# A modulated filter chain on one core: the blur taken out of the filter's matmuls

## The reference

```python
def _layer(x, style, w, b, mw, mb, typ):
    s = style @ mw.T + mb
    weight = SCALE * w * s[:, None, :, None]
    demod = lax.rsqrt(jnp.sum(weight * weight, axis=(2, 3)) + EPS)
    weight = weight * demod[:, :, None, None]
    if typ == 'same':
        out = jax.vmap(_conv_same)(x, weight) + b[None, :, None]
    elif typ == 'upsample':
        out = jax.vmap(_conv_up)(x, weight.transpose(0, 2, 1, 3)) + b[None, :, None]
        out = _blur(out, 2.0 * blur_k, (1, 1))
    elif typ == 'downsample':
        xb = _blur(x, blur_k, (2, 2))
        out = jax.vmap(_conv_down)(xb, weight) + b[None, :, None]
    return out
# types in order: same, upsample, same, downsample; blur_k = [1, 3, 3, 1] / 8
```

## Time and profile before

| | us |
|---|---|
| median of three runs | 1350.0 |
| the profiled execution, first to last instruction | 1349.2 |
| TensorE busy in it | 1342.2 |
| VectorE busy | 1077.1 |
| ScalarE busy | 818.2 |
| GpSimd busy | 330.2 |
| DMA moved | 141.32 MB, mean 105 GB/s |

### The profile page before, as it was taken

The page is one execution under the profiler, slowest core; times in us unless marked ns, Lnnn a source line. Parts: engine busy times, 40 slices in busy tenths (PEclk is TensorE's granted clock), DMA queues, the critical chain, the costliest instruction groups (busy, mean ns, idle before and its releaser), DMA issues.

```text
span 1349.2 us, 20544 instructions
## 1 busy us (share of the span) xinstructions
PE 1342.2 (99%) x7013; PEld 1128.4 (84%) x7013; DVE 1077.1 (80%) x1798; ACT 818.2 (61%) x1407; POOL 330.2 (24%) x633
## 2 busy tenths in 40 slices
PE   8999999999999999999999999999999999999999
PEld 7888888888888888888888888888888888888887
DVE  7978788887787888878778788787777777777775
ACT  7755556556565565565665556656557577676674
POOL 3243211141312212205222122121422242222210
PEclk9999999999999999999999999999999999999999
DMA  7333133321333213333223332233332053123311
GB/s 237 139 117 105 60 119 110 118 99 69 116 117 110 100 61 114 118 110 126 78 87 118 102 118 79 87 118 118 118 117 87 1 162 136 66 100 118 118 47 71
DMA packets 75447, 141.32 MB, mean 105 GB/s; under 512 B 6800, under 2 KB 8592, under 8 KB 75344
## 3 DMA queue, kind: packets, MB, share of 16 engines
q1 hardware_dynamic: 74976, 139.73, 30.3%
q10 hardware_dynamic: 368, 0.28, 0.1%
HBM read 72.40 MB, written 67.24 MB: 103 GB/s over the span
## 4 chain that ended last, share of the span: by engine, by line
PE 99%; DVE 0%; issue 0%; ACT 0%; ACTq 0%
PE ps L456 97%; PE ps L579 1%; PE ps L388 1%; PE ps L436 0%; PE ps L410 0%; DVE vf L1028 0%; ACT vh L765 0%; DVE vh L1035 0%; DVE gp L1053 0%; DVE zl L998 0%; DVE X L1018 0%; DVE xl L992 0%; DVE gp L1049 0%; ACT scr L808 0%; DVE scr L903 0%
## 5 line engine op out<-in xcount | busy, mean ns | idle before, releaser
L744 ACT ACTIVATE zh<-ps,t_bx 128x512 fp32r<-128x512 f32 x256 | 175.4, 685 | 460.5 <-PE ps L456 458.8
L456 PE MATMUL ps<-zh,gh 128*128 128x512 f32 (+1 forms) x1028 | 406.6, 396 | 1.6 <-DVE gh L1173 1.5
L456 PE MATMUL ps<-zl,gh 128*128 128x512 f32 (+1 forms) x1028 | 405.0, 394 | 0.0
L456 PE MATMUL ps<-zh,gl 128*128 128x512 f32 (+1 forms) x1028 | 281.4, 394 | 0.0
L998 DVE SCALAR_TENSOR_TENSOR zl<-ps,t_bx,zh 128x512 fp32r<-128x512 f32 x256 | 190.3, 743 | 55.3 <-ACT zh L744 55.2
L456 PEld LDWEIGHTS ps<-zh,gh 128*128 128x128 f32 x1028 | 193.6, 188 | 45.7 <-issue 2.4
L456 PEld LDWEIGHTS ps<-zh,gl 128*128 128x128 f32 x1028 | 193.5, 188 | 44.9
L456 PEld LDWEIGHTS ps<-zl,gh 128*128 128x128 f32 x1028 | 193.7, 188 | 42.5
L992 DVE SCALAR_TENSOR_TENSOR xl<-X,t_S,xh 128x513 fp32r<-128x513 f32 x256 | 201.3, 786 | 18.9 <-ACT xh L732 13.2
L1284 POOL TENSOR_TENSOR w3h<-w3q,w3h 64x256 fp32r<-64x256 f32 x63 | 49.2, 780 | 624.7 <-ACT w3h L758 621.4
L1007 DVE SCALAR_TENSOR_TENSOR X<-ps,t_D,X 128x512 f32<-128x512 f32 x255 | 189.4, 743 | 4.1 <-PE ps L456 4.0
(11 more groups left out here) (207 smaller groups left out, 1977.5 us busy)
## 6 DMA issues: line engine op xcount, KB each, us to landing
out_x<-X SPq DMA_DIRECT2D x255, 256.5 KB, 2.8
X<-out_x SPq DMA_DIRECT2D x96, 513.0 KB, 6.5
X<-x_in SPq DMA_DIRECT2D x32, 513.0 KB, 6.4
pk<-taps_in SPq DMA_DIRECT2D x3, 512.0 KB, 11.5
pk<-pack_in SPq DMA_DIRECT2D x3, 352.0 KB, 11.6
pk<-sets_in SPq DMA_DIRECT2D x4, 256.0 KB, 3.5
pk<-taps_in SPq DMA_DIRECT2D x2, 96.0 KB, 3.6
w3f<-w_in SPq DMA_DIRECT2D x1, 192.0 KB, 9.0
```

What stands on the lines that cost most here:

```text
L456: return pe.matmul(out_ap, a, b, start=first, stop=last, skip_group_check=True)
L744: act.activation(zh[n % 2][:, ZPAD:ZPAD + M], ps[:, ZP + n % 2, :], IDENT, bias=tab["bx"][:, k, b:b + 1]).then_inc(s["zhi"], 1)
```

## The change

- Layer 1's weights go into the filter's matmuls without the blur. w1h and w1l (four slots: the three taps and a zero, shifted by one on the lower rows) and w1d and w1dl (the same taps on both halves, the rounding and the low part) replace rh, rl, rd, rdl. k_products has 16 products where g_products had 21; v's last part carries its high part on the upper and its low part on the lower rows of one tile (vh slot 2), so vends is gone. k_products stands at the start of step n = 4q - 4, ahead of conv0(n+1).
- ScalarE evicts the seven raw sums k0 to k6 from PSUM with the scale T1s = T1 / 32 (kev: eight copies a quad, two per sample, four ahead of zhi(n+1) and four behind it) into kp, two samples on the upper rows and two on the lower.
- In the next step VectorE blurs: the filter (1, 6, 15, 20, 15, 6, 1) as seven operations over both pairs (fir_even ahead of zlo(n+1), fir_odd behind it, then xlo(n+3)). gf holds the seven taps.
- One step on, ScalarE rounds gf into sh (ghi) and VectorE takes the low part into sl (glo), 896 elements a row each; SyncE copies both by DMA to gh and gl, each to the upper rows and, one slot on, to the lower ones (spread, eight copies a quad, waiting on ScalarE and VectorE). convg waits for these DMAs. Samples 0 and 1 are made by copies on the engines.
- w3hi runs one step earlier, vlo and the second half of the old order are moved (vfull behind zlo, vlo one step later), v_products(1) stands before the loop.
- The setup of the blurred weights (R_TAP0 to R_TAP2, SPLIT_R) and the copies rd<-rh, rdl<-rl, rl<-rl are gone; w1hi (ScalarE, three copies) and SPLIT_1 (VectorE, three subtractions; for the first block on GpSimd, ahead of w0l) come in.

```diff
-            def g_products(q):
-                pairs = ((inner, 4, 0), (inner, 3, 1), (fifth, 5, 1))
-                alone = ((inner, 1, 4), (fifth, 3, 4), (split, 0, 3))
...
+            def k_products(q):
+                k6, k45, k23, k01 = (ps[:, VG + i // 2, i % 2 * QS * C:(i % 2 + 1) * QS * C] for i in range(4))
+                early, late = slice(0, 2), slice(2, 4)
+                pairs = ((k01, early, 0), (k23, late, 0), (k23, early, 1), (k45, late, 1))
+                pe.wait_ge(s["w1l"], k + 1)
+                pe.wait_ge(s["vh"], q + 1)
+                for i, (at, w, o) in enumerate(pairs):
+                    add(at, h[:, w, :], vh[:, o, :, :], first=i in (0, 3))
+                    add(at, l[:, w, :], vh[:, o, :, :])
+                pe.wait_ge(s["vlp"], q + 1)
+                for at, w, o in pairs:
+                    add(at, h[:, w, :], vl[:, o, :, :])
+                pe.wait_ge(s["vl"], q + 1)
+                add(k45, d[:, early, :], vh[:, 2, :, :])
+                add(k45, dl[:, early, :], vh[:, 2, :, :])
+                add(k6, d[:, late, :], vh[:, 2, :, :])
+                add(k6, dl[:, late, :], vh[:, 2, :, :]).then_inc(s["K"], 1)
...
+            def spread(q):
+                first, second = 2 * q, 2 * q + 1
+                for name, ready, of, to in (("ghd", "gsh", sh, gh), ("gld", "gsl", sl, gl)):
+                    sp.wait_ge(s[ready], q + 1)
+                    for h, rows in ((first, slice(0, C)), (second, slice(C, 128))):
+                        if q == 0 and h == first:
+                            continue
+                        if h >= 3:
+                            sp.wait_ge(s["convg"], 2 * (h - 2))
+                        src = of[rows, :, :, :].bitcast(F32)
+                        sp.dma_start(to[0:C, h % 3, :, 0:NT, :].bitcast(F32), src).then_inc(s[name], 16)
+                        sp.dma_start(to[C:128, h % 3, :, 1:NT + 1, :].bitcast(F32), src).then_inc(s[name], 16)
...
             for n in range(NN + 4):
+                if n == 2:
+                    spread(0)
+                if n - 2 >= 0 and n - 2 < NN and g_at(n - 2) is not None:
+                    spread(g_at(n - 2))
...
+            def evict(q, j, part):
+                rows, i = slice(j // 2 * C, (j // 2 + 1) * C), j % 2
+                got = ps[:, VG:VG + 2, :].rearrange("p k (r s c) -> p (k r) s c", r=2, c=C)
+                of, to, r = ((slice(0, C), EVEN, 0), (slice(C, 128), ODD, 1))[part]
+                return act.activation(kp[rows, to, i, :], got[of, r:, j, :], ACT.Copy, scale=tab["T1s"][of, k, b:b + 1])
...
+            def fir_even(rows, i):
+                step(dve.scalar_tensor_tensor(gf[rows, 1:5, i, :], kp[rows, 1:8:2, i, :], BLUR_O, kp[rows, 3:10:2, i, :],
+                                              ALU.mult, ALU.add))
+                step(dve.scalar_tensor_tensor(gf[rows, 5, i, :], kp[rows, 7, i, :], BLUR_O, kp[rows, 5, i, :], ALU.mult, ALU.add))
+                settle()
+                step(more(rows, i, slice(2, 5), slice(1, 6, 2), BLUR_O))
+                settle()
+                step(dve.tensor_tensor(gf[rows, 3:5, i, :], gf[rows, 3:5, i, :], kp[rows, 1:4:2, i, :], ALU.add))
+            def fir_odd(rows, i):
+                settle()
+                step(more(rows, i, slice(1, 4), ODD, BLUR_E))
+                settle()
+                step(more(rows, i, slice(2, 5), ODD, BLUR_M))
+                settle()
+                return more(rows, i, slice(3, 6), ODD, BLUR_E)
...
             for n in range(2, NN):
-                if n + 3 < NN:
+                due = g_at(n - 1)
+                if due is None and n + 3 < NN:
                     xlo(n + 3)
                 xnew(n - 1)
+                if due is not None:
+                    dve.wait_ge(s["kev"], due + 1)
+                    dve.wait_ge(s["gsh"], due)
+                    fir_even(whole, both)
                 if n + 1 < NN:
                     zlo(n + 1)
+                if due is not None:
+                    fir_odd(whole, both).then_inc(s["fir"], 1)
+                    if n + 3 < NN:
+                        xlo(n + 3)
                 if v_at(n - 1) is not None:
+                    vfull(v_at(n - 1))
+                if g_at(n - 2) is not None:
+                    glo(g_at(n - 2))
```

More of the change, by code:

```diff
@@ L67 @@
 ENDS = ((0, 1), (M - 2, M - 1), (M - 1, M))
-def blur_table():
-    t = np.zeros((2 * C, NJ * K), np.float32)
-    for half in range(2):
-        for j in range(NJ):
-            for c in range(K):
-                i = 2 * j - 8 - half + 4 + c
-                if -6 <= 2 * j - 8 - half <= 2 and 0 <= i < 7:
-                    t[half * C:(half + 1) * C, j * K + c] = ALLBLUR[i] / 32.0
-    return t
 def edge_tables():
@@ L625, in _ @@
             conv0(0)
-            g_products(0)
+            pe.wait_ge(s["z0"], 1)
+            k_products(0)
             conv0(1)
-            pe.wait_ge(s["z0"], 1)
+            v_products(1)
             for n in range(NN):
+                if g_at(n) is not None and n not in G_LATE:
+                    k_products(g_at(n))
                 if n == 0:
@@ L638, in _ @@
                     setup(0, BIAS_U)
-                if g_at(n) is not None and n not in G_LATE:
-                    g_products(g_at(n))
                 k, stage = edge_at(n)
@@ L838, in _ @@
             xhi(1)
-            vends(0)
+            w3hi(1)
             zhi(0)
+            act.wait_ge(s["K"], 1)
+            act.wait_ge(s["t1s"], 1)
+            for j in (0, 2, 1, 3):
+                evict(0, j, 0)
+                ins = evict(0, j, 1)
+                if j == 2:
+                    ins.then_inc(s["kev0"], 1)
+            ins.then_inc(s["kev"], 1)
             ghi_first(0)
-            w3hi(1)
             xhi(2)
@@ L845, in _ @@
             ghi_first(1)
-            ghi(1)
+            ghi_rest()
             vhi(1)
+            xhi(3)
             root(PARTS[2], 3)
             zhi(2)
-            vends(1)
-            xhi(3)
             xhi(4)
-            gl_shifted(1)
+            kev(1, 0)
+            kev(1, 1)
             w3hi(2)
             for n in range(2, NN):
-                if n > 2 and v_at(n - 2) is not None:
-                    vends(v_at(n - 2))
                 if n + 3 < NN:
                     xhi(n + 3)
+                if g_at(n) is not None:
+                    kev(g_at(n), 0)
                 if n + 1 < NN:
                     zhi(n + 1)
-                for half in range(2):
-                    if n - 1 - half >= 0 and g_at(n - 1 - half) is not None:
-                        ghi(2 * g_at(n - 1 - half) + half)
+                if g_at(n) is not None:
+                    kev(g_at(n), 1)
+                if g_at(n - 2) is not None:
+                    ghi(g_at(n - 2))
                 if v_at(n - 1) is not None:
@@ L869, in _ @@
                     setup(k, stage)
-                if v_at(n + 1) is not None:
-                    w3hi(v_at(n + 1))
+                if v_at(n + 2) is not None:
+                    w3hi(v_at(n + 2))
                 if where(n)[1] == NBLK - 1:
@@ new lines, in step, with settle, more @@
+            def step(ins):
+                chain[0] += 1
+                ins.then_inc(s["dve_set"], 1)
+            def settle():
+                dve.wait_ge(s["dve_set"], chain[0])
+            def more(rows, i, to, of, factor):
+                dve_out = gf[rows, to, i, :]
+                return dve.scalar_tensor_tensor(dve_out, kp[rows, of, i, :], factor, dve_out, ALU.mult, ALU.add)
+            def fir_even(rows, i):
[6 more added lines that the diff above has]
+                step(dve.tensor_tensor(gf[rows, 3:5, i, :], gf[rows, 3:5, i, :], kp[rows, 1:4:2, i, :], ALU.add))
@@ L1209, in _ @@
                     setup(0, BIAS_U)
-                for half in range(2):
-                    if n - 1 - half >= 0 and g_at(n - 1 - half) is not None:
-                        glo(2 * g_at(n - 1 - half) + half)
-                if v_at(n) is not None:
-                    vfull(v_at(n))
-                if g_at(n) is not None:
-                    gscale(g_at(n)).then_inc(s["gp"], 1)
             xlast()
@@ new lines, in _ @@
+            for a in (w1h, w1l):
+                link(pool.memset(a[0:C, :, K, :].bitcast(F32), 0.0))
+                link(pool.memset(a[C:128, :, 0, :].bitcast(F32), 0.0))
+            for a in (w1d, w1dl):
+                link(pool.memset(a[:, :, K, :].bitcast(F32), 0.0))
+            sig(pool.memset(kp[:, NONE], 0.0), "kz")
+            sig(pool.memset(ye[0:C, Q_R1, :], 0.0), "z0")
+            pool.wait_ge(s["w1hi"], 1)
+            pool.wait_ge(s["w1t"], 16)
+            fence()
+            hi, own = w1h[:, 0].bitcast(F32), w1d[:, 0].bitcast(F32)
```

350 lines of the change are left out of this document (131 added, 219 removed), and 2 rows, old and new, of the table s.

## The result

The changed kernel takes **1391.8 us** in the median of four runs (1389.66 to 1394.57); the kernel before, on the same chip, 1349.8 (1349.14 to 1350.95). The ratio is 1.0311, 95% interval 1.0297 to 1.0326: 3.1% slower, where 1327 was predicted and the range ended at 1343. The profiled execution of after spans 1392.7 us, 43.5 more than before's 1349.2; it is the longest of the four, 2.8 us above their median, so sums from the trace come out a little larger than those from the medians.

What follows compares the result with a forecast made beforehand. TensorE's matmul stream was taken as the bound: 1349.2 - 36.9 (matmuls) + 9 (start) + 3 (block boundaries) + 2 (mild late low parts) = 1326.3 us profiled, 1327 as median; range 1317 to 1343.

Steps and rivals of the forecast that it cites:

- The matmuls, -36.9: TensorE's filter block: 16 products instead of 21, 0.119 us each, saving 0.595 us a quad over 62 quads, -36.9 us.
- VectorE and ScalarE per quad: Per quad, VectorE loses 6.0 us and gains 5.4; ScalarE loses 5.2 and gains 4.9; neither becomes the bound.
- The new chain by its due times: From T, TensorE's start of the step after the filter products: vlo ends T+13.6, read at T+14.7, 1.1 us spare.
- Copies by DMA: SyncE's eight copies a quad, 2.7 us each: issued from T+9.0, last lands T+16.3, due T+19.0, 2.7 us spare.
- Rival 3: Copies land late behind loads and convg waits; 5.3 us in every second quad would give 1497 us; chance 0.05.
- Rival 2: VectorE's low parts late every quad, held up beside GpSimd's w3lo and w3s; 0.8 us a quad gives 1377; chance 0.14.
- no bound either: ScalarE's 4.9 us of added work a quad sets no limit, even in the last block's extra 0.7 us pass per sample.
- The start, +9: First two quads and start-up chain: +8.3 us, then some 0.7 at the next filter block; bounds 4 and 14.
- w0l behind w1l: On GpSimd at the start, w0l stands behind three subtractions of w1l: conv0(0) ends near 16.9, not 15.9.
- spread(0) behind the store: On SyncE at the start, spread(0) is issued near 39.6; two copies land near 42.7, when convg(2) starts, before at 34.45.
- rival 1: Start dearer: TensorE idles in several places, its clock falls to 1.2 GHz, 1333 to 1338 us; chance 0.11.
- Block boundaries, +3: w3hi one step earlier makes ScalarE wait for w3q: 0.7 us of TensorE idle each time, +3 us for four blocks.

Runs made afterwards that it cites:

- section 4: Changed kernel with two start orders changed: GpSimd makes w0l ahead of w1l and w1dl, SyncE issues the first quad's copies ahead of sample 0's store; 1386.7 us.
- section 5: Kernel with the copies' order, vlo's place and the start's two orders mended, plus GpSimd's edge_apply put three samples later, behind w3s and w3lo; 1329.3 us.

## Why the prediction was wrong, step by step

- **The matmuls, -36.9: right.** -35.4 in the run that only leaves them out; a filter block takes 1.97 us.
- **VectorE and ScalarE per quad: right in size.** The evictions take 0.46 and 0.41 us (0.47 and 0.42 estimated), the rounding copies 0.41 and 0.95, the blur's 128x384 0.57. Over the run VectorE's busy time fell by 29.6 us and ScalarE's by 46.1.
- **The new chain by its due times: right up to the copies.** sh was ready at T+9.0 and sl at T+10.3, as worked out. The cover of vlo was thinner than the 1.1 us: undisturbed, in quad 8, it ended 0.43 us behind the start of the filter block, where its products are due 0.95 behind, so 0.5 us.
- **Copies by DMA: the step that failed, 38 us.** It took each copy as landing 2.7 us after its own issue, as if eight could travel at once. The landings show them one after another: issued at T+9.0, the first lands 2.9 us later and the other seven in 7.5 us behind it, at T+19.4 where T+19.0 was due. The 2.7 us to spare were not there: 37 waits, and 0.62 us a quad lost (29.6 us from K4 to K52 by the new order, and 4.6 behind K63), as much as the products bring. Some 5 us of that are one place of the profiled execution, a wait of 3.2 us ahead of 278.58 with the lower clock behind it, where quad 12 takes 26.6 us (21.8 in the kernel of section 4). The prediction had the number for it in hand, from the Trainium skill, SBUF - State Buffer, "Door 1: The DMA port swizzle": 229,376 B at the 218 GB/s of that section are an estimated 1.05 us, and the trace agrees in size (1.00 to 1.03 us for five of the seven steps, 223 to 229 GB/s). Whether the ports are the reason no run here tells. The prediction asked what one copy costs by it, not what eight in a row do.
- **Rival 3** was therefore the true mechanism, with its price from the copies themselves. It had looked for lateness in the loads ahead of them, and there it gave it 5 in 100; that form came up once (section 5).
- **Rival 2: right in its mechanism**, GpSimd's w3lo beside vlo, 1.11 us for 0.70. In blocks 0 to 2 the 0.5 us of cover absorbed most of it (7.7 us in 48 quads with the copies mended, which the earlier vlo gave back). In the last block "no bound either" for ScalarE missed a wait: xb comes ahead of xhi, VectorE's xlo stands at the head of its queue for it, and vlo behind it lost the rest of its cover. 18 us in all, and of the last block's 10.3 half goes with the short xb. The Trainium skill, SBUF - State Buffer, "SBUF: two separate sides", says that a VectorE operation with two SBUF inputs and a GpSimd operation that reads SBUF exclude each other. The trace agrees in kind, with 0.4 to 0.6 us more for a VectorE subtraction beside a GpSimd one of 0.7 to 0.8; that the first to come keeps the port for its whole instruction no run here tells.
- **The start, +9: mis-sized.** K4 came 16.5 us late where the prediction's terms give 7.8 (9 less the 1.2 that K2 and K3 save). Two of its steps were seen, w0l behind w1l and spread(0) behind the store, but convg(2) came at 45.39, not 42.7. K4 starts at 102.4 in after, at 95.8 with the start's orders mended, at 97.0 with the copies' order, at 93.0 with all mends, 7.1 later than in the kernel before: part of the excess was the copies again. TensorE's granted clock fell to the lower of its two levels, 1.2 GHz, at 14.6 us, in a gap of 2.37 us that followed one of 1.31, and K(0) took 3.4 us rather than 1.9 (0.83 is the mean granted clock of the first 30 us): **rival 1** came true beside the others, with some 30 us of the whole run at that level. It didn't take a gap of 3 us: at 65.8 us the clock fell again, and the gaps ahead of that were 1.30 us (to 61.05) and 1.99 (to 65.14). The prediction's own evidence against it was weaker than it looked: the 1.00 of the earlier trace rows has no record of the clock ahead of 14.2 us, and there the kernel before ran its products of 256 columns 0.21 us apart (11.49 to 13.41), against 0.12 from 15.90 on.
- **Block boundaries, +3: wrong.** ScalarE's waits for w3q did grow, from 15.1 to 50.6 us, but they didn't reach TensorE: with the other causes gone, K4 to K52, with all three boundaries in it, takes 973.3 us, as in the kernel with the products alone left out (973.5). In their place stands the one at quads 52 to 55, 5.9 us, from transfers ahead of the copies.

With the copies' order, vlo's place and the start's two orders mended the kernel takes 1331.6 us, 5 above the forecast. That is another kernel than the one forecast, so it doesn't make the forecast right.

## What to carry to other kernels

Cost a series of DMA copies as the first one's latency and then one step for each that follows (here 1.0 us for 229,376 B), and set the last against its due time; then order them by when they are needed, which here was worth 37.5 us of 1392 without one byte less. When an in-order queue has a wait at its head, ask what behind it does not need that wait: a subtraction moved into the idle time was worth 18 us, while moving the other engine's work away from it cost 9. And a mend that brings little by itself (5.7 us at most) can bring three times that once another limit in the same place is gone.

## What the runs showed of the hardware

- Copies of 229,376 B (128 pieces of 1,792 B) from 64 rows of SBUF to 64, back to back on one queue, land every 1.00 to 1.09 us behind a first step of 1.37 (changed kernel, 524.83 to 532.35 us); of 114,688 B (64 pieces) every 0.40 to 0.46 us. SyncE's issue of one takes 0.6 us for the first three, 0.6 to 1.1 behind them, and up to 2.4 where eight stores and four loads lie ahead (1107.32 us in the kernel of section 5).
- Behind eight stores and four loads (4.2 MB, issued in the 11 us before) such a copy lands 10.3 to 12.0 us after its issue; with the loads behind the copies 3.2 to 5.4 in the same place.
- VectorE subtractions with two SBUF inputs beside a GpSimd subtraction: 128x512 1.10 to 1.26 us for 0.69, 64x256 1.00 for 0.42 (changed kernel); a 128x384 multiply-add up to 1.97 for 0.56 (w3hi a step later).
- TensorE's granted clock fell to its lower level at 65.8 us in the changed kernel, behind gaps of 1.30 and 1.99 us.
